# A fused attention and expert layer on one core: a new order for the last half, jobs that begin behind the values, and products moved from DVE to ACT

## What is computed

```python
# first block: attention over layer-normed rows; masked scores count as 0, not as minus infinity
qkv = einsum('bhce,ef->bhcf', heads(layernorm(x)), Wqkv) + bqkv
att = softmax((q @ k.T / sqrt(8)) * tril(ones, k=-1))
x   = x + (att @ v) @ Wr + br
# second block: rotary causal attention, then two of eight experts
xn  = layernorm(x)
q_in = k_in = rope(xn); v_in = xn
ctx = softmax(causal(q @ k.T / sqrt(8))) @ v
x1  = layer_norm(xn + ctx @ out_proj_w.T + out_proj_b)        # ln1
gates = softmax(x1 @ gate_w.T + gate_b); top 2 are kept
moe = sum over the two of gate * (x1 @ expert_w[e].T + expert_b[e])
out = x + layer_norm(x1 + moe)                                 # ln2
```

## Time and profile before

| | us |
|---|---|
| median of 3 runs (808.70 to 813.13) | 811.14 |
| the profiled execution | 811.19 |
| its span | 809.4 |
| from the start to the first exponential | 32.25 |
| the last values end, the tail begins | about 741.4 |
| busy: PE, ACT, DVE, POOL | 675.6, 631.3, 412.3, 325.1 |

### The profile page before, as it was taken

One profiled execution on the slowest core, in us unless ns is written; L12 is line 12 of the kernel. 1 busy time (PEld: TensorE's weight loads), 2 busy tenths in 40 slices (PEclk: granted clock), 3 DMA queues, 4 the chain that ended last, 5 costly groups with the idle time before them and its releaser, 6 DMA issues. The chain is left out here.

```text
span 809.4 us, 15701 instructions
## 1 busy us (share of the span) xinstructions
PE 675.6 (83%) x5752; PEld 283.5 (35%) x5752; DVE 412.3 (51%) x1115; ACT 631.3 (78%) x665; POOL 325.1 (40%) x635
## 2 busy tenths in 40 slices
PE   3589988898898978988998889898878889898644
PEld 2334333333333333333343334233323234334533
DVE  4465352355453742484465643635524533755875
ACT  1389989999797996998898899897798988985000
POOL 3162226323532433532753346425542245534233
PEclk9799999999899998999999999999999999999756
DMA  5766367445655344333464424431473433310000
GB/s 136 264 207 221 96 208 271 138 127 177 202 199 189 131 161 114 114 106 105 136 198 157 157 83 147 124 113 67 134 223 125 139 98 129 97 64 1 26 27 15
DMA packets 76994, 109.81 MB, mean 136 GB/s; under 512 B 13784, under 2 KB 28256, under 8 KB 76896
## 3 DMA queue, kind: packets, MB, share of 16 engines
q1 hardware_dynamic: 73232, 107.85, 41.9%
q10 hardware_dynamic: 3664, 0.77, 0.5%
HBM read 60.91 MB, written 47.68 MB: 134 GB/s over the span
## 5 line engine op out<-in xcount | busy, mean ns | idle before, releaser
L1281 ACT ACTIVATE probs<-scores,shift 128x1024 f32<-128x1024 f32 x576 | 598.6, 1123 | 94.9 <-PE scores L1107 90.1
L1357 POOL TENSOR_SCALAR_AFFINE_SELECT probs<-probs 128x256 f32<-128x256 f32 (+1 forms) x448 | 200.6, 465 | 366.2 <-ACT probs L1281 365.6
L1136 PE MATMUL acc<-probs,v 128*9 128x512 f32 (+3 forms) x3072 | 319.2, 503 | 1.3 <-ACT num L1224 1.0
L1107 PE MATMUL scores<-qs,ks 32*128 32x512 f32 (+3 forms) x1536 | 158.8, 428 | 59.0 <-ACT probs L1281 57.1
L1107 PEld LDWEIGHTS scores<-qs,ks 32*128 32x128 f32 x1536 | 72.3, 187 | 211.1 <-ACT probs L1281 139.4
L1136 PEld LDWEIGHTS acc<-probs,v 128*9 128x9 f32 x3072 | 58.9, 100 | 96.3 <-issue 64.7
L1397 DVE TENSOR_TENSOR prod<-side,G 128x512 f32<-128x512 f32 x47 | 32.5, 691 | 86.9 <-PE side L1089 81.5
L1089 PE MATMUL side<-we,x1T 128*128 128x256 f32 x188 | 66.7, 438 | 4.4 <-DVE prod L1397 4.4
L1089 PEld LDWEIGHTS side<-we,x1T 128*128 128x128 f32 x188 | 28.9, 192 | 49.0 <-issue 27.0
L1338 POOL TENSOR_TENSOR moe<-psum 128x256 f32<-128x256 f32 x32 | 24.7, 770 | 48.1 <-DVE x1b L1397 29.4
L1224 ACT ACTIVATE num<-acc 128x512 f32<-128x512 f32 x64 | 38.5, 601 | 6.5 <-PE scores L1010 4.3
(11 more groups left out here) (177 smaller groups left out, 638.2 us busy)
## 6 DMA issues: line engine op xcount, KB each, us to landing
ks<-k_dram SPq DMA_DIRECT2D x96, 256.0 KB, 4.2
q_dram<-part SPq DMA_DIRECT2D x64, 256.0 KB, 3.1
qs<-q_dram SPq DMA_DIRECT2D x64, 256.0 KB, 3.2
num_dram<-num SPq DMA_DIRECT2D x60, 256.0 KB, 3.1
k_dram<-part SPq DMA_DIRECT2D x32, 256.0 KB, 3.6
xrow<-in_x SPq DMA_DIRECT2D x16, 256.0 KB, 4.4
nat<-num_dram SPq DMA_DIRECT2D x15, 256.0 KB
rdenb<-rden_dram SPq DMA_DIRECT2D x15, 256.0 KB
```

The source lines that it names most:

```text
L1107: ins = pe.matmul(scores[:, pair(g, h // 2), h % 2, col:col + w], ks[u][r, kt // TH, (kt % TH) * P:(kt % TH + 1) * P], qs[u][r, q0:q0 + w] ...
L1136: ins = pe.matmul(acc[h * VW:h * VW + VC, q0:q0 + w], v9[V_OF[k]][:, kt, :, HG * hg + h], src, start=(s == 0), stop=last, skip_group_check ...
L1281: act.activation(dst, src, ACT.Exp, bias=shift[:, column(k):column(k) + 1], scale=SCALE).then_inc(probs_raw, 1)
L1357: ins = pool.affine_select(out=blocks, in_=blocks, compare_op=ALU.is_ge, fill=0.0, base=a - 1, pattern=[[0, blocks.shape[1]], [1, P]], cha ...
```

## The change

Six edits. In the head the two statistics come before `pairs`, and the first `xT` before `bound`; PE no longer waits for `bv` (DVE waits for it at the first `v`); ACT writes the first of the two parts of each `k` of batch 0, and issues the two DMAs that store the first `k`. In the loop a job of two pieces begins only at an odd point, behind the values, unless it is one of p2. In the tail the planner lets PE run ahead of DVE by up to seven jobs as soon as the operands are there, and lets DVE choose between the oldest of these and its own turns by the longest way that is left. And there ACT makes the `e1` products, four instructions of 128x128 each.

```diff
-            out[("p3", b, "e0", t)] = [x("pick3")]
+            out[("p3", b, "e0", t)] = [x("pick3"), ("p3", *((b, "e1", t - 1) if t else (b - 1, "e1", T - 1)))]
-        ends[x("store")] = at(k + 2, 40 if j else 0)
+        ends[x("store")] = at(k + 2, 40 * j)
...
-BEFORE_TURNS = ([("p0", 0, "pairs", 0), ("p1", 0, "stats", 0), ("p1", 0, "stats", 1), ("p1", 0, "root", 0), ("p1", 0, "root", 1),
-                 ("p1", 0, "rows", 0), ("p0", 0, "bound", 0), ("p1", 0, "rows", 1), ("p1", 0, "xT", 0), ("p0", 0, "roots", 0),
+BEFORE_TURNS = ([("p1", 0, "stats", 0), ("p1", 0, "root", 0), ("p1", 0, "stats", 1), ("p1", 0, "root", 1), ("p0", 0, "pairs", 0),
+                 ("p1", 0, "rows", 0), ("p1", 0, "xT", 0), ("p0", 0, "bound", 0), ("p1", 0, "rows", 1), ("p0", 0, "roots", 0),
...
+    def operands(x, t):
+        if x[2] in ("e0", "e1"):
+            if (x[1], x[3] // TH) != LAST_HALF[1:]:
+                return ready(x, t, NPOINT)
+            before = [y for y in waits[x] if y[2] in ("e0", "e1")] + [(*x[0:2], "bias", (x[3] - 2) // TH)]
+            if any(y not in jobs for y in before):
+                return False
+            return done.get((*x[0:2], "x1T", x[3] // TH), 1e9) <= t
+        return ready(x, t, NPOINT)
...
-            x = next((x for x in pending if x[2] in PIECES and ready(x, t, p)), None)
+            x = next((x for x in pending if x[2] in PIECES and ready(x, t, p) and (p % 2 or PIECES[x[2]] == 1 or x[0] == "p2")), None)
...
+    def left(x):
+        if x not in way:
+            way[x] = takes(x) + max([left(y) for y in followers[x]], default=0.0)
+        return way[x]
+    pending.sort(key=left, reverse=True)
...
+        if clock["PE"] <= t and (len(jobs) < first + 2 * PAIRS + 1 or banks[-1] <= t or len(begun) < 2 * PAIRS):
+            x = next((x for x in pending if x[2] in PIECES and operands(x, t)), None)
+            if x and len(begun) < 2 * PAIRS + 1:
+                jobs.append(x)
...
+        if clock["DVE"] <= t:
+            x = next((x for x in pending if x[2] not in PIECES and turn_time(x)[0] == "DVE" and ready(x, t, NPOINT)), None)
+            if begun and begun[0][1] <= t and ready(begun[0][0], t, NPOINT) and (x is None or left(begun[0][0]) > left(x)):
+                x, _end = begun.pop(0)
...
+BY_ACT_ORDER = [x[:4] for x in AFTER if x[2] == "e1" and x[5]]
+K_BY_ACT = [x[:4] for x in BEFORE if x[2] == "k" and x[5]]
...
-        n_first = len(FIRST) + 1
+        n_first = len(FIRST)
...
+                if (work, b, name, i) in K_BY_ACT:
+                    act.wait_ge(side_done, done((work, b, name, i)))
+                    act.activation(part[part_count(0, b, i) % 2][:, 1, 0, :], bank_of((work, b, name, i)), ACT.Identity, bias=bqk[:, 1:2]).then_inc(act_parts, 1)
+                if (work, b, name, i) == ("p1", 0, "parts_out", 0):
+                    k_out(act, 0, b, i)
...
+                if (work, b, name, i) in BY_ACT:
+                    act.wait_ge(G_ready, 2 * b + i // TH + 1)
+                    act.wait_ge(side_done, done((work, b, name, i)))
+                    act.wait_ge(products_ready, b * T + i)
+                    src = bank_of((work, b, name, i)).rearrange("p (e d) -> p e d", d=D)
+                    for e in range(NE // 2):
+                        ins = act.activation(prod[:, 1, e, :], src[:, e, :], ACT.Copy, scale=G[i // TH][:, i % TH, NE // 2 + e:NE // 2 + e + 1])
+                    ins.then_inc(act_products, 1)
...
+                        if job in BY_ACT:
+                            dve.wait_ge(act_products, BY_ACT_ORDER.index(job) + 1)
+                            dve.wait_ge(side_free, done(job) - 1)
+                            dve.sem_inc(side_free, 1)
```

More of the change, by code:

```diff
@@ L423, in schedule @@
     t = clock["PE"]
-    while pending:
+    begun = []
+    way = {}
+    def left(x):
[3 more added lines that the diff above has]
+    pending.sort(key=left, reverse=True)
+    first = len(jobs)
+    while pending or begun:
         at_point.append([])
         others(t, NPOINT, False)
-        others(t, NPOINT, True)
-        x = next((x for x in pending if x[2] in PIECES and ready(x, t, NPOINT)), None)
-        if x and (len(banks) < 2 * PAIRS + 1 or banks[-2 * PAIRS - 1] <= t):
-            jobs.append(x)
-            n, pe, _free, _dve = JOB_TIMES[x[2]]
-            for c in range(n):
-                place(x, t, c)
-            t += n * pe
-            clock["PE"] = t
-            finish(x)
-        else:
-            t += 0.1
@@ L743, in half_block, with k_out @@
             return h if pair(g, 0) < pair(g, 1) else (h + 2) % HG
+        def k_out(engine, a, b, j):
+            engine.wait_ge(side_free, done((("p1", "p2")[a], b, "k", j)))
+            use = part_count(a, b, j)
+            for d in range(2):
+                engine.dma_start(k_d[a][b, j, :, :, d].rearrange("h e s -> (h e) s"),
+                                 part[use % 2][:, 1, d, :].bitcast(F32)).then_inc(part_out[use % 2], 16)
         block = ctx.enter_context(nc.Block())
@@ L826, in parts_out @@
                                      pt[:, 0, i, :].bitcast(F32)).then_inc(part_out[use % 2], 16)
-                for d in range(2):
-                    sp.dma_start(k_d[a][b, j, :, :, d].rearrange("h e s -> (h e) s"),
-                                 pt[:, 1, d, :].bitcast(F32)).then_inc(part_out[use % 2], 16)
+                if (a, b, j) != (0, 0, 0):
+                    k_out(sp, a, b, j)
             def sums(a, b, name, i):
@@ L1441, in project @@
                             dve.wait_ge(sq_ready, 2 * b0 + j0 + 1)
-                    link(dve.tensor_scalar(pt[:, c, 0, :], src, bias[:, c:c + 1], None, ALU.add))
+                    if job in K_BY_ACT:
+                        dve.wait_ge(act_parts, K_BY_ACT.index(job) + 1)
+                    else:
+                        link(dve.tensor_scalar(pt[:, c, 0, :], src, bias[:, c:c + 1], None, ALU.add))
                     ins = dve.scalar_tensor_tensor(out=pt[:, c, 1, :], in0=src, scalar=bias[:, c:c + 1], in1=pt[:, c, 0, :],
```

36 lines of the change are left out of this document (32 added, 4 removed).

## The result

The changed kernel takes 822.3 us (median of 4 runs, 815.19 to 825.12), the kernel before took 809.92 on the same chip (median of 4, 806.88 to 813.13): a ratio of 1.0147, with a 95% interval of 1.0097 to 1.0197. It is slower by 1.5%, where 799 and a gain of 1.5% were forecast. The profiled execution took 820.87 us, 1.8 above its span of 819.1. In all that follows a run more than 1.5% above the fastest of its kernel counts in the median but not in the ratio and its interval: three of the twelve runs of norm_later, and one each of loop_only and loop_old.

What follows compares the result with a forecast made beforehand. ACT was taken to bound the loop, PE hard behind; chains of DVE, PE and POOL the tail, of loads, DVE and PE the head. 811.2 - 4.8 - 3.7 - 3.5 = 799.2, said as 799; range 791 to 809.

Steps and rivals of the forecast that it cites:

- The loop: Loop: the new order of jobs cuts ACT's waits on scores, -3.7 us, bounds -10 and +8.
- my sum of 73.0: Loop: ACT's waits as mean wait per class of groups times their new counts, 73.0 us against 76.7.
- slower: new waits for `side`: Rival, loop: jobs beginning right behind another make PE stand; five new waits of 2 to 4 us, +15, 818 us; chance 0.08.
- The head: Head: earlier statistics and rows bring the first scores forward, -4.8 us, bounds -5.7 and -2.0.
- the old one: Head: behind the normalised rows, 4.5 us earlier, the chain was taken to run as in the kernel before.
- The gain of 1.1 for stores issued side by side: Head: with `k`'s two stores issued beside `q`'s four, the last issue begins some 1.1 us earlier.
- the head does half of it: Rival, head: weights land at 8.7 and the second half runs at half speed; -2 to -2.8, 802 us; chance 0.14.
- The tail: Tail: PE running ahead and ACT's products shorten it, -3.5 us, bounds -7 and +2.5.
- the marks of the earlier trace: Tail: `att` ready, `out` read, x1 ready, the gates, last sum begins; forecast shifts +1.7, +6.5, -0.5, +0.2, -1.8 us.
- The rival of a clock that stays up: Rival, tail: running ahead fills the gap before the gates, full clock behind it, tail -7; 795 or 792 us; chance 0.16.
- the tail gives nothing: Rival, tail: `out` 6.5 us late is not won back, tail +2.5, loop 0, 809 us; chance 0.12.
- ACT's products: Tail: four ACT copies of 128 columns take 1.0 us, freeing 0.69 on DVE ten times; 1.9 a tile against 2.3.

Runs made afterwards that it cites:

- norm_later: Changed kernel with one `norm` job of the loop moved from point 86 to 87 and the `q` there one point later: 814.42 us, ratio 1.0037 to the kernel before.
- loop_only: Kernel before with both edits of the loop's order alone, old head and old tail: 820.74 us, ratio 1.0104 to the kernel before.
- loop_old: Changed kernel without both edits of the loop's order, new head and new tail kept: 805.89 us, ratio 0.9937 to the kernel before.
- head_only: Kernel before with the head's edits alone: 805.47 us, ratio 0.9919 to the kernel before.
- tail_only: Kernel before with the tail's new planner and ACT's products alone: 811.66 us, ratio 1.0026 to the kernel before.
- head_loop: Changed kernel with the old planner of the tail and all products on DVE: 815.41 us, ratio 1.0101 to the kernel before.
- head_again: Kernel before with the head's edits alone, a repeat of head_only: 805.48 us, ratio 0.9959 to the kernel before.

## Why the prediction was wrong, step by step

**The loop, -3.7 forecast, +10.4 measured.** This is the step that failed, and its sign was wrong. I took the mean wait of each class of groups and counted classes. Two of the means held: groups with a piece behind the values waited 0.112 us (0.10 taken), those with one before them 0.181 (0.17). But the 40 groups with both waited 0.68 instead of 0.40, since three of them are above 2 us: 27.1 us where my term had 16.1, which is 11 of the 14.8 between my sum of 73.0 and the 87.8 measured. (That sum also counts 64 short groups where 63 have a group behind them; with 63 it is 72.5.) I named the gap myself ("a means-only account misses single long waits"), priced it as noise of +-8 around zero, and kept the gain as the value. It is not noise: the same wait comes back in each kernel with this order, and which job stands before which wait could be read from the order. What the account lacked altogether is the clock. PE's waits in line for `side` jobs grew only from 23.3 to 27.5 us, ACT's waits by 11.1; at group 44 the clock shows as 1.75 of 4.28. How the rest of the 11.1 divides between waits in line and clock is not shown. The order costs in the tail too, where it leaves two more jobs; these the forecast had in its marks of the tail.

**The rival "slower: new waits for `side`"** was right in kind, with a chance of 0.08. It wanted 12 us of new long waiting; it was 12.4. It named five new waits of 2 to 4 us, and there were six more above 1.5. It stopped at 818 since it credited head and tail in full. Its price is that of waits for DVE, while the longest one is for POOL's squares; "POOL late" stands in the forecast's passage on long waits.

**The head, -4.8.** Right in nine of the eleven executions with the new head, and 2.1 in the profiled one. The statistics start at 4.04, rows and `q`, `k` 5.1 us sooner than in the earlier trace rows. Timeline of the changed kernel:

```profile
4.04 0.87 DVE L1477 BATCH_NORM_STATS2 stats<-xrow 128x6 f32<-128x128 f32 x4 [2.58 <-DMA xrow<-in_x]
...
6.48 0.21 PE L1092 MATMUL scores<-pairs 8*9 8x9 f32 x2 [6.48 <-DMA bqk<-in_bqk]
...
10.29 3.78 PE L1025 MATMUL scores<-xT,wqkv 128*128 128x256 f32 x8 [0.27 <-DVE xT L1502]
...
13.63 0.20 ACT L1299 ACTIVATE clw<-c2w 128x1 f32<-128x1 f32 x1 [7.50 <-issue]
...
14.92 0.73 DVE L1517 TENSOR_SCALAR part<-scores,bqk 128x512 fp32r<-128x512 f32 x1
...
17.12 2.92 SPq L884 DMA_DIRECT2D q_dram<-part  x4
17.12 0.85 ACTq L801 DMA_DIRECT2D k_dram<-part  x2
...
17.84 3.65 PE L1025 MATMUL scores<-xT,wqkv 128*128 128x256 f32 x8 [2.16 <-DVE xT L1502]
...
23.20 0.32 SPq L816 DMA_DIRECT2D qs<-q_dram  x1
...
26.81 1.16 PE L1106 MATMUL side<-later,v 128*128 128x128 f32 x8 [1.54 <-DVE sfx L1683]
...
29.24 0.80 PE L1165 MATMUL scores<-qs,ks 32*128 32x512 f32 x4 [1.28 <-issue]
```

The loads begin 3.5 us sooner, not 5.7. Of `q` and `k`'s 5.1 only 3.65 reach the stores (17.12 against 20.77). DVE takes up `q` at 14.92, 4.6 us after PE began it, where it was 2.1 before: the steps of `roots` stand ahead of it and wait for ACT, which takes its first step (`clw`) only at 13.63, behind its own DMA issues. I had called this chain "the old one". The gain of 1.1 for stores issued side by side did not come either: from the first store's issue to the first load it is 6.08 us, before it was 5.91. SyncE's four issues took 2.92 us instead of 1.79. In this execution the first exponential is at 30.16; in nine of the ten others with the new head it is at 27.2 to 27.9, 4.3 to 5.0 sooner than before, as forecast (norm_later, the tenth, 29.8). What sets these two apart is the clock: PE stood 2.16 us for the second `xT`, the clock was at half from 17.9 to 21.3, and the second half's `q` and `k` took 3.65 us. The same matmuls at the full clock, in the changed kernel's second run:

```profile
17.50 1.97 PE L1025 MATMUL scores<-xT,wqkv 128*128 128x256 f32 x8 [1.75 <-DVE xT L1502]
```

That is the second condition of the rival "the head does half of it", which the prediction had at 0.14; its first, weights that land at 8.7, did not come (`bqk` lets PE begin at 6.48). The length of the wait alone does not decide it: head_only stood 2.59 us at this place and kept the full clock.

What I had no term for either is that part of the lead is given back at once, where batch 1's rows are late.

**The tail, -3.5 forecast, +1.5 measured, and nothing in tail_only.** Behind the same new order of the loop, head_loop's tail with the old planner takes 71.8 us, as the changed kernel's does. Counted from the end of the last values, the marks of the earlier trace rows move from 11.0, 18.3, 31.7, 43.5 and 58.4 to 13.7, 26.3, 32.0, 44.2 and 59.9. Forecast were 12.7, 24.8, 31.2, 43.7 and 56.6. Four of the five are within 1.5 us; the last leg took 15.7 instead of 12.9. PE in the changed kernel's tail:

```profile
781.63 0.63 PE L1122 MATMUL scores<-ident,x 128*128 128x128 f32 x4 [4.22 <-DVE x L1494]
...
793.78 0.60 PE L1134 MATMUL side<-ident,G 128*8 128x128 f32 x4 [2.11 <-DVE G L1469]
800.12 2.04 PE L1141 MATMUL scores<-be,GT 8*128 8x128 f32 x8 [5.74 <-DVE GT L1755]
802.09 5.83 PE L1147 MATMUL scores<-we,x1T 128*128 128x256 f32 x16
```

```profile
796.20:806.20 10.00, 6.08 (x18) 5.08 (x19) 4.96 (x9) 1.38 (x5) 2.80 (x6) 0.50 0.21 56
```

PE ran ahead and then stood 5.74 us for the copy of `GT`, which DVE reached behind products, sums and batch 2's last steps. The clock fell there, so the bias took 2.04 and the last four products 5.83, where I had counted 1.1 and 4.2: 2.6 us, nearly the whole miss of this leg. The gap before the gates did close, from 5.96 to 2.11 us, and a new one opened behind them. The rival of a clock that stays up was wrong for that reason, and the argument for "the tail gives nothing" (five jobs behind the late copy of `GT`) was the right one. I also took 2 us off because adding up the old order ran long. It did not for the new one: without that correction the last mark would have stood at its -1.8, still better than what came.

**ACT's products**, 1.0 us taken for four:

```profile
L1314 ACT ACTIVATE prod<-scores,G 128x128 f32<-128x128 f32 x40 | 11.4, 368 | 38.1 <-PE scores L1147 29.1
...
769.14 1.14 ACT L1314 ACTIVATE prod<-scores,G 128x128 f32<-128x128 f32 x4 [9.34 <-PE scores L1147]
```

(the page, then the timeline). One takes 368 ns, but four that follow each other are through in 1.14 us, for they overlap. The value from the rows was 0.14 short. The 1.6 us estimated from the Trainium skill ("ScalarE: Activation LUTs", Rules for kernel authors) were 0.46 too much; for a single one the same rule gives an estimated 0.41, near the 0.368 measured.

**My own marks** said wrong if the first exponential comes after 30 (30.16), if ACT's single waits above 1.5 us sum to over 25 (29.7), or if x1 comes after 776 (781.63). All three came true, but two of them not for what they were set to catch. 30.16 is this execution's; in the changed kernel's second run it is 27.71. And x1 comes after 776 because the tail began 8.2 us later, not because of the tail itself: counted from there it is 32.0 us, 0.8 more than forecast. The second mark told why: it asks for the single long waits. ACT's waits on scores, forecast near 68, were 84.9.

## What to carry to other kernels

Before an order is changed in a loop that one engine bounds, list the jobs for which another engine stands in line, and ask of each what its operand's producer does at the new place; means over classes say nothing about them, and one job of hundreds was worth 0.35% in one kernel and 0.7 to 1.1% in the other. A wait of TensorE can cost more than its length where the granted clock falls in it, 1.75 us on top of 2.53 here: look at the clock in the window behind each wait. Count what an order leaves undone for the next stage. Try the parts of a change singly: the head's edits alone, 0.992 and 0.996, beat both kernels, and the whole hid it.

## What was not expected of the hardware

- TensorE's clock fell to half inside a loop in which PE was busy for 88% of the time, a microsecond into a wait of 2.2 us (from 123.7, the wait from 122.8 to 125.0). The same place with a wait of 1.22, or with matmuls in the wait, kept the full clock. But in the head a wait of 2.16 was followed by half clock in two executions and one of 2.59 in a third was not.
- Stores issued by two engines at the same moment landed no sooner: 6.08 us from the first issue to the first load that needs them, against 5.91 with SyncE alone. Why, no run separates: SyncE's four issues took 2.92 us beside ACT's two and 1.79 alone, but the second half's four took 2.76 alone in the kernel before.
- A run of this kernel has a spread of about 1% that goes with its granted clock: 4.8 us between the lower and the upper half of head_again's runs, whose clocks differ by about 0.01.
